# A two-layer adapter block on one core: the x product one tile further ahead of the experts, the bias product ahead of the first transpose, one quarter of the experts' low parts one routing later

## What is computed

```python
y   = x @ W.T + b + 2.0 * (x @ lora_As[slot]) @ lora_Bs[slot]    # slot per sequence
h   = y @ A.T                       # 64 values per row
p   = softmax(y @ router_w.T)       # 16 experts, the two largest kept, divided by their sum
out = x + y @ base_w.T + base_b + 0.5 * sum_e combine[e] * (h @ B[e].T)
```

## Time and profile before

| | |
|---|---|
| runs of the kernel (3) | 103.42, 103.99, 104.17 us, median 103.99 |
| the profiled execution's own time | 102.98 us |
| its span | 101.2 us |
| granted TensorE clock, mean over the span | 1.00 |
| TensorE matmul busy | 97.4 us, 96% |
| TensorE weight loads busy | 88.1 us, 87% |
| VectorE / ScalarE / GpSimd busy | 66.5 / 41.4 / 21.3 us |

### The profile page before, as it was taken

The page is one execution under the profiler, slowest core; times in us unless marked ns, Lnnn a source line. Parts: engine busy times, 40 slices in busy tenths (PEclk is TensorE's granted clock), DMA queues, the critical chain, the costliest instruction groups (busy, mean ns, idle before and its releaser), DMA issues.

```text
span 101.2 us, 1808 instructions
## 1 busy us (share of the span) xinstructions
PE 97.4 (96%) x572; PEld 88.1 (87%) x572; DVE 66.5 (66%) x184; ACT 41.4 (41%) x100; POOL 21.3 (21%) x34
## 2 busy tenths in 40 slices
PE   6999999999999999999999999999999999999990
PEld 7799999999999899789988997899787787788980
DVE  5729996999389776949917946676468626648101
ACT  1705445878768626554344127110910603012000
POOL 5100002243999970070430050000000000000000
PEclk9999999999999999999999999999999999999999
DMA  2999459999955083386196091470074091750211
GB/s 42 362 363 378 138 111 313 366 410 424 314 118 97 23 220 66 115 185 196 23 254 219 16 266 37 126 198 3 16 188 141 5 268 60 216 198 0 104 58 52
DMA packets 8155, 16.92 MB, mean 167 GB/s; under 512 B 1539, under 2 KB 3971, under 8 KB 8018
## 3 DMA queue, kind: packets, MB, share of 16 engines
q1 hardware_dynamic: 7474, 16.41, 53.2%
q10 hardware_dynamic: 640, 0.40, 1.3%
q0 software_dynamic: 32, 0.00, 0.0%
HBM read 13.28 MB, written 2.16 MB: 153 GB/s over the span
## 4 chain that ended last, share of the span: by engine, by line
PE 93%; DMA 3%; DVE 0%; ACT 0%; issue 0%
PE pair L804 89%; DMA w_raw_all<-w_cat 3%; PE pair L963 1%; PE pair L943 1%; PE pair L945 1%; DVE xn L798 0%; PE pair L920 0%; ACT w_hi_all L416 0%; PE pair L933 0%; PE pair L922 0%; PE pair L912 0%
## 5 line engine op out<-in xcount | busy, mean ns | idle before, releaser
L804 PE MATMUL pair<-e_hi,w_hi_all 128*128 128x512 f32 (+1 forms) x72 | 27.3, 379 | 0.0
L804 PE MATMUL pair<-e_hi,w_lo_all 128*128 128x512 f32 (+1 forms) x72 | 26.7, 370 | 0.0
L804 PE MATMUL pair<-e_lo,w_hi_all 128*128 128x512 f32 (+1 forms) x72 | 26.6, 370 | 0.0
L742 DVE TENSOR_TENSOR exp_raw_all<-w_raw_all 128x512 f32<-128x512 f32 x16 | 10.3, 687 | 10.7 <-DMA w_raw_all<-spill 10.7
L526 ACT ACTIVATE w_hi_all<-exp_raw_all 128x512 fp32r<-128x512 f32 x16 | 9.7, 629 | 15.8 <-DVE exp_raw_all L742 15.8
L804 PEld LDWEIGHTS pair<-e_hi,w_lo_all 128*128 128x128 f32 x72 | 13.6, 188 | 2.5
L804 PEld LDWEIGHTS pair<-e_hi,w_hi_all 128*128 128x128 f32 x72 | 13.6, 189 | 2.4
L804 PEld LDWEIGHTS pair<-e_lo,w_hi_all 128*128 128x128 f32 x72 | 13.6, 189 | 1.8
L749 DVE TENSOR_TENSOR w_lo_all<-exp_raw_all,w_hi_all 128x512 fp32r<-128x512 f32 x16 | 10.4, 689 | 3.1 <-ACT w_hi_all L526 2.5
L804 PE MATMUL pair<-p_hi,w_hi_all 128*128 128x304 f32 x32 | 9.8, 307 | 0.0
L804 PE MATMUL pair<-p_hi,x_hi 128*128 128x304 f32 x32 | 9.8, 305 | 0.0
(11 more groups left out here) (106 smaller groups left out, 166.9 us busy)
## 6 DMA issues: line engine op xcount, KB each, us to landing
w_raw_all<-spill SPq DMA_DIRECT2D x16, 256.0 KB, 3.9
exp_raw_all<-experts SPq DMA_DIRECT2D x4, 512.0 KB, 8.4
xn<-x_n SPq DMA_DIRECT2D x4, 512.0 KB, 7.4
out<-xn SPq DMA_DIRECT2D x7, 256.0 KB, 3.9
w_raw_all<-w_cat SPq DMA_DIRECT2D x3, 552.0 KB, 7.0
xt_raw<-x_t SPq DMA_DIRECT2D x2, 512.0 KB, 7.0
xt_raw<-x_t SPq DMA_DIRECT2D x1, 1024.0 KB, 12.4
c_stack<-c_hi SPq DMA_DIRECT2D x7, 74.0 KB, 4.4
```

What stands on the lines that cost most here:

```text
L742: nc.vector.tensor_tensor(g[:, js, :], weight_rows[:, b, js, :], hidden[:, b, :].unsqueeze(1).to_broadcast([P, GH, P]), ALU.mult).then_inc ...
L804: return nc.tensor.matmul(out_ap, lhs, rhs, start=first, stop=last)
```

## The change

Five edits. (1) TensorE has a whole further x product ahead of the experts: `x_other(4)`, `routing_transpose(2)`, `x_first(5)`, `lora_product(4)` move ahead of the loop, and each iteration works on tiles one further; the orders of ScalarE and VectorE follow. (2) `bias()` stands ahead of `lora_first_transpose()`, and ScalarE reads its result ahead of the transposed values. (3) VectorE's quarter of `e_lo` stands behind `route(1)`, where it stood behind `route(0)`. (4) The load of the residual rows of tiles 4 and 5 is issued ahead of the first `spread_routing`. (5) For row block k = 1 of W the high part is made in two pieces of 256 columns, with a semaphore of its own for the first (`wh_next`), and TensorE waits for each piece where it needs it.

```diff
         wh_left = sem("wh_left")
+        wh_next = sem("wh_next")
         wh_done = sem("wh_done")
...
+            load_residual(2)
             spread_routing(0)
             stack_rows(5)
             spread_routing(1)
-            load_residual(2)
...
-            for k in range(1, KC):
+            act.wait_ge(in_w[1], 16)
+            for cols, done in ((W_LEFT, wh_next), (W_RIGHT, wh_done)):
+                nc.scalar.activation(w_hi[:, 1, cols], w_raw[:, 1, cols], ACT.Copy).then_inc(done, 1)
+            for k in range(2, KC):
...
-            lora_first_t()
             act.wait_ge(pe_bias, 1)
             nc.scalar.activation(bias_hi[F_BIAS:FT, :], w2_cols(ps_b)[F_BIAS:FT, :], ACT.Copy).then_inc(bh_done, 1)
+            lora_first_t()
...
             routing_rows(1)
+            x_hi_part(5)
+            lora_hi(4)
+            exps(3)
+            routing_rows(2)
             g_hi(0, 0)
             g_hi(0, 1)
-            lora_hi(4)
-            exps(3)
+            lora_hi(5)
+            exps(4)
             for t in range(NT - 1):
+                if t + 6 < NT:
+                    x_hi_part(t + 6)
                 if t + 5 < NT:
-                    x_hi_part(t + 5)
-                if t + 4 < NT:
-                    routing_rows(t + 2)
+                    routing_rows(t + 3)
...
             route(0)
-            split_experts_lo(2)
             lora_lo(2)
             read_z(1)
             route(1)
+            split_experts_lo(2)
             lora_lo(3)
             read_z(2)
             route(2)
+            lora_lo(4)
+            read_z(3)
+            route(3)
             weigh(0, 0)
             weigh(0, 1)
             g_lo(0, 0)
             g_lo(0, 1)
-            lora_lo(4)
-            read_z(3)
-            route(3)
+            lora_lo(5)
+            read_z(4)
+            route(4)
...
-                pe.wait_ge(wh_done, k + 1)
                 pe.wait_ge(wh_first, k + 2)
                 for m in range(KC):
+                    if k == 1 and m == 0:
+                        pe.wait_ge(wh_next, 1)
+                    elif m == (KC // 2 if k == 1 else 0):
+                        pe.wait_ge(wh_done, k + 1)
                     fold_pass(m, k, w_hi, w_hi, False, False)
...
-                if t + 4 < NT:
-                    x_other(t + 4)
+                if t + 5 < NT:
+                    x_other(t + 5)
...
-                if t + 4 < NT:
-                    routing_transpose(t + 2)
+                if t + 5 < NT:
+                    routing_transpose(t + 3)
...
-                if NT - 2 <= t + NB < NT:
-                    routing_transpose(t + NB)
+                if NT - 2 <= t + 4 < NT:
+                    routing_transpose(t + 4)
...
-                if t + 4 < NT:
-                    lora_product(t + 4)
+                if t + 5 < NT:
+                    lora_product(t + 5)
...
-                if t + 5 < NT:
-                    x_first(t + 5)
+                if t + 6 < NT:
+                    x_first(t + 6)
...
+            bias()
             lora_first_transpose()
-            bias()
...
             lora_product(3)
+            x_other(4)
+            routing_transpose(2)
+            x_first(5)
+            lora_product(4)
```

More of the change, by code:

```diff
@@ L553, in _ @@
             routing_rows(1)
+            x_hi_part(5)
+            lora_hi(4)
+            exps(3)
+            routing_rows(2)
             g_hi(0, 0)
             g_hi(0, 1)
-            lora_hi(4)
-            exps(3)
+            lora_hi(5)
+            exps(4)
             for t in range(NT - 1):
+                if t + 6 < NT:
+                    x_hi_part(t + 6)
                 if t + 5 < NT:
-                    x_hi_part(t + 5)
-                if t + 4 < NT:
-                    routing_rows(t + 2)
+                    routing_rows(t + 3)
                 g_hi(t + 1, 0)
                 g_hi(t + 1, 1)
-                if NT - 2 <= t + NB < NT:
-                    routing_rows(t + NB)
-                if t + 4 < NT:
-                    exps(t + 4)
+                if NT - 2 <= t + 4 < NT:
+                    routing_rows(t + 4)
                 if t + 5 < NT:
-                    lora_hi(t + 5)
+                    exps(t + 5)
+                if t + 6 < NT:
+                    lora_hi(t + 6)
         @block.vector
@@ L787, in _ @@
                 g_lo(t + 1, 1)
-                if t + 4 < NT:
-                    read_z(t + 4)
-                    route(t + 4)
                 if t + 5 < NT:
-                    lora_lo(t + 5)
+                    read_z(t + 5)
+                    route(t + 5)
+                if t + 6 < NT:
+                    lora_lo(t + 6)
             finish(NT - 2)
```

## The result

| | before | after |
|---|---|---|
| median of 22 runs each | 103.05 us | 102.42 us |
| lowest, highest | 102.19, 104.80 | 101.68, 103.66 |
| ratio, 95% interval | | 0.994, 0.9919 to 0.9961 |
| profiled execution, its span | 102.98, 101.2 | 102.43, 100.0 |

The change makes the kernel 0.6% faster. What put it there is the base: the median of 103.99 came from three runs, and over 22 runs, those three among them, the same kernel has 103.05. The gain itself is 0.63 us where 0.33 was forecast.

A forecast was written before the change was run, and what follows sets the result against it. TensorE, busy 97.4 of 101.2 us, was taken as the bound. Terms 0.12 + 0.29 - 0.2 + 0.12 = 0.33 us gained took the median of 103.99 to 103.66 us, range 102.6 to 104.5.

The forecast's parts named there:

- The two holes at tiles 0 and 3: TensorE's lost time ahead of tile 0's adapter product, 0.19 us, and ahead of tile 3's x product, 0.29 us.
- The first expert started without a wait: TensorE reaches the first expert at 44.8 us, `g_lo(0)` is done at 44.15: cost 0, 0.65 us to spare.
- the rival of 107.5: Residual rows ahead of the spill delay the first `weigh`; the first expert waits 3.8 us, time 107.5 us; chance 0.09.
- The verdict "no change that can be told at 1%": For the whole kernel, a time within 1% (1.04 us) of before was called likeliest, chance 0.78.
- the wait at tile 4: Ahead of tile 4's x product, moving `e_lo` opens a new TensorE wait of 0.2 us, bounds 0 and 0.75.
- The paragraph on the engines' turns: At tile 4, VectorE and GpSimd alternate whole instructions; by that rule no new wait, and a sum 0.2 us larger.
- The first hole: Ahead of tile 0's adapter product: putting the bias product before the transpose gains 0.12 us, bounds 0 and 0.19.
- the third hole: Ahead of the transpose of routing 2, at 41.91 to 42.26 us: 0.12 us lost, expected to go entirely.
- I apply the difference to the median: The gain, summed against the profiled 102.98 us, was taken off the runs' median of 103.99 us.
- five tiles ahead: Extra x product before the first expert: gains 0.12 us at the transpose of routing 2; new waits cost 0, bound 0.3.
- the rival that put the 1.01 us between runs and profile on slack overrun: Late spreads overrun the tail's 0.7 us slack in timed runs; earlier routing removes those waits, giving 102.65 us; chance 0.13.
- the row block in two pieces: At row block k = 1, nothing waits, so no gain; two pieces cost less than 2 x 0.64 us; cost 0.

## Why the prediction was right and wrong

**Right.** TensorE's stream sets the end, and nothing was added to it. The two holes at tiles 0 and 3 were rightly read and rightly put down to VectorE, and the undone edit 3 brings the second back (0.41). The first expert started without a wait, at 44.18 where 44.8 was forecast (0.6 of it is the earlier start of that profile). The 512 KB ahead of the spill, the rival of 107.5, did no harm: the read back was issued 3.26 us behind the spill (31.58 to 34.84) instead of 2.30, up to 4.16 in the kernel with the order alone, and the first `weigh` did not wait in any profile of the new order. The weights landed 0.6 us later than before, where 1 to 2 was expected. The verdict "no change that can be told at 1%" is what was measured.

**Wrong: the wait at tile 4.** The sum took 0.2 off for it, since x's low part might lose 0.92 beside `e_lo`. It lost nothing: the subtraction ahead of it was blocked instead, x's low part ran 35.03 to 36.32, and TensorE came at 36.71. The term measured 0. Without it the sum is 0.53, within the interval of the measured 0.63 (0.40 to 0.83), which 0.33 is not. The paragraph on the engines' turns had this value; the sum did not use it. The first hole gave 0.10 for 0.12. That 0.53 comes so near the 0.63 is in part luck, since one of its terms, the third hole of 0.12, stands in one of six profiles of the old order only.

**Wrong: the base. This is the step that failed.** "I apply the difference to the median" hung the forecast and its range on 103.99, the median of three runs, and nothing was allowed for its own uncertainty. The same kernel has 103.05 over 22, 0.94 lower, which is more than the 0.60 of all three holes. On that base the forecast is 102.72 with a range from 101.7. With the old base even the gain as measured gives 103.99 - 0.63 = 103.36, inside the range: the base, and not the terms of the sum, put 102.42 outside. (The forecast of 103.66 was also written down as 103.6, not 103.7, which changes nothing here.)

**Wrong in kind: "five tiles ahead" as the smallest of three terms.** I gave it 0.12 us, for the third hole, and wrote that the first expert has 0.65 to spare in the new order, but I did not ask how much it had in the old one. It had 0.02: 39.13 + 2.23 = 41.36, a DMA's landing and three instructions behind it, for a TensorE that could start at 41.20 + 0.14 = 41.34. In the earlier trace rows the idle time of 0.66 "<-DMA" ahead of `weigh` hints at it. TensorE came late enough for the wait to be invisible, because its first matmuls were slow in that profile, because of the very holes that the change closes, and because the way from the spill to `weigh` was the shortest of six profiles. So the holes were not three terms that add up. With the old order, closing them moves the wait to the first expert and gives nothing: L - S is 89.95, 90.24 and 90.13 with one or three of the edits, against 89.85. From the issue of the spill to `weigh` it takes 6.9 to 7.4 us in the six profiles of the old order. With the new order a further 3.6 us of x's product lie over it, and every hole that is closed counts: 89.58 with the `e_lo` hole, 89.24 without. This is shown in profiles; the times bear out the new order against the old one, but not that the small edits are worth nothing without it.

This also answers the rival that put the 1.01 us between runs and profile on slack overrun. There was next to nothing to explain: 0.94 of the 1.01 was the small sample. Other profiles do wait where this one does not, but at the first expert, at 41 us, and not in the tail, and their last add comes no later for it (97.66 to 98.53, against 98.57).

**Half wrong: the row block in two pieces.** "Nothing waits" was true of the profile read and not of others: where TensorE is early, block 1 starts 0.56 behind the landing and not 0.68. The two pieces together took 0.72 us, not near 2 x 0.64.

What stays open: the share of each edit in the timed 0.6%. Intervals of four tenths of a per cent do not part terms of 0.1 to 0.3 us; what is shown of them is shown in profiles.

## What to carry to other kernels

Closing a hole in the bounding engine's stream is worth something only up to the next place where that engine would have to wait for something else. Before adding up holes, look for the next place where a helper's row has idle time ended by a DMA, work out from the helper's chain when the bounding engine could start there, and compare it with when it did; equality to a few hundredths of a us, as 41.36 here, means a wall that the trace does not mark as a wait. And check in a second profile that a hole is there at all. And a base of three runs with a spread of 0.7% is no base for a range of one per cent: the level's own uncertainty belongs in the range.

## What the runs showed of the hardware

- Two subtractions from SBUF, one on VectorE and one on GpSimd, do not run side by side: 2.18 to 2.37 us for 1024 columns on VectorE when GpSimd was in the middle of one, 1.22 when VectorE started first, and 0.32 us became 1.28 on GpSimd behind a VectorE one. Where the pair meets decides more than what it costs.
- TensorE's first matmuls in the fold, of 296 columns, step by 0.25 us and then by 0.14 us, and change over at 4.5 to 6.8 us, differently from profile to profile, behind the same 13 matmuls on zeros (0.79 to 3.91, 0.24 us each). The granted clock column reads 1.00 for the whole of both, but the trace's own record of the clock begins only at 6.88 us in the profile before and at 4.50 us in that after, at 1.00, just where the steps change, and the column counts the time without a record as full. By an estimate from the step, 296 columns in 0.247 us are 1.2 per ns, the lower of the clock's two levels. Between the profiles before and after the start of block 1 moved by 0.6 us.
- The last part of the time varies behind the last add: it is 2.6 us to the end of the span in the kernels before and after, and 4.0 in the profile of the kernel with edits 2, 3 and 5 (102.2 - 98.17), whose last store took 3.1 us to land against 1.7. So some of the scatter of the runs can lie outside the computation.
